# Moving background dequantisation further into the middle layers, and running the last feed-forward by token halves, in a four-layer transformer kernel

## The reference, cut to what matters

```python
x = x + L0_xattn(layernorm(x), ctx)   # 16 heads of 96, 64 context keys + 256 own keys per batch
x = x + L0_ffn(layernorm(x))          # silu(gate/128) * up, 512 -> 1376 -> 512, truncated to int8 twice
x = x + L1_xattn(layernorm(x), ctx)   # one head, softmax(x ctx^T) ctx
x = x + L1_ffn(layernorm(x))          # 64 experts of rank 8, 16 taken per token by a router
x = x + L2_xattn(layernorm(x), ctx)   # as layer 1, with Wq, Wk and biases
x = x + L2_ffn(layernorm(x))          # 3 experts 512 -> 512 -> 512 (tanh, gelu, silu), gated per token
x = x + L3_xattn(layernorm(x), ctx)   # RMS norm with a weight ln_w, 32 heads of 16, grouped keys
x = x + L3_ffn(layernorm(x))          # silu(x dq1^T) * (x dq2^T), then dq3^T; 512 -> 1376 -> 512
...
def nf4_quant_dequant(w):             # dq1..3: blocks of 64 share a maximum; 16 code values
    absmax = jnp.max(jnp.abs(flat), axis=1, keepdims=True)
    idx = jnp.searchsorted(bounds, flat / absmax)
    return (NF4_CODE[idx] * absmax).reshape(shape)
```

## Time and profile before

| | |
|---|---|
| median of 3 runs | 1513.26 us (1510.02 to 1513.64) |
| profiled execution | 1513.1 us, span of its instructions 1511.4 us |
| mean granted TensorE clock | 0.949 |
| TensorE busy | 1366.7 us, 90% of the span |
| VectorE busy | 1002.1 us, 66% |
| GpSimd busy | 328.1 us, 22% |

### The profile page before, as it was taken

The page is one execution under the profiler, slowest core; times in us unless marked ns, Lnnn a source line. Parts: engine busy times, 40 slices in busy tenths (PEclk is TensorE's granted clock), DMA queues, the critical chain, the costliest instruction groups (busy, mean ns, idle before and its releaser), DMA issues.

```text
span 1511.4 us, 18615 instructions
## 1 busy us (share of the span) xinstructions
PE 1366.7 (90%) x6429; PEld 1055.8 (70%) x6429; DVE 1002.1 (66%) x2200; ACT 474.3 (31%) x1004; POOL 328.1 (22%) x187
## 2 busy tenths in 40 slices
PE   6689999999999989997797889778999899999998
PEld 5467676777676766886675676556887677778886
DVE  3577878767878667876988667675446777444242
ACT  3333334333324233341344141322221443321010
POOL 4101211112111111342224140214443230012120
PEclk9889999999999999999899799879999999899999
DMA  4412433323322222332322220100112000011001
GB/s 153 144 39 77 112 116 111 107 77 95 90 80 78 68 77 83 86 113 86 109 81 82 85 84 1 56 29 16 43 54 70 28 29 2 1 49 63 25 20 56
DMA packets 112559, 104.86 MB, mean 69 GB/s; under 512 B 14674, under 2 KB 84194, under 8 KB 112466
## 3 DMA queue, kind: packets, MB, share of 16 engines
q1 hardware_dynamic: 111954, 102.81, 23.2%
q0 software_dynamic: 512, 0.85, 0.2%
HBM read 92.79 MB, written 10.82 MB: 69 GB/s over the span
## 4 chain that ended last, share of the span: by engine, by line
PE 67%; DVE 18%; DMA 4%; issue 3%; ACT 3%; SPq 3%; POOL 2%; ACTq 0%; DVEq 0%
PE bank L1724 49%; PE bank L2093 5%; PE bank L1818 4%; DVE nf_y L1664 4%; PE bank L2028 2%; PE bank L2048 2%; PE bank L1808 2%; POOL slots L858 2%; DVE xn L1238 1%; SPq L807 1%; PE bank L1751 1%; SPq L792 1%; ACT slots L951 1%; PE bank L2037 1%; DVE nf_w L1658 1%
## 5 line engine op out<-in xcount | busy, mean ns | idle before, releaser
L858 POOL TENSOR_TENSOR slots<-staging,slots 128x1024 fp32r<-128x1024 f32 (+5 forms) x114 | 269.0, 2364 | 1025.7 <-ACT slots L951 1025.7
L1724 PE MATMUL bank<-xT,slots 128*128 128x512 f32 (+1 forms) x1920 | 462.0, 398 | 4.5 <-DVE xT L1247 3.2
L1724 PEld LDWEIGHTS bank<-xT,slots 128*128 128x128 f32 (+1 forms) x1920 | 349.0, 183 | 103.5 <-issue 10.8
L1664 DVE TENSOR_SCALAR nf_y<-nf_w 128x512 fp32r<-128x512 f32 (+2 forms) x495 | 254.1, 550 | 21.1 <-PE bank L2093 20.0
L951 ACT ACTIVATE slots<-staging 128x1024 fp32r<-128x1024 f32 (+5 forms) x114 | 115.2, 1018 | 251.1 <-PE bank L1724 217.5
L2093 PE MATMUL bank<-nf_y,nf_d 128*128 128x512 f32 (+2 forms) x495 | 160.9, 418 | 36.2 <-DVE nf_y L1664 20.5
L1724 PE MATMUL bank<-slots,h 128*128 128x512 f32 (+1 forms) x728 | 178.9, 406 | 0.7 <-POOL slots L858 0.7
L1724 PEld LDWEIGHTS bank<-slots,h 128*128 128x128 f32 (+1 forms) x728 | 141.3, 195 | 36.3 <-issue 1.8
L2093 PEld LDWEIGHTS bank<-nf_y,nf_d 128*128 128x128 f32 (+1 forms) x495 | 92.1, 192 | 75.0 <-DVE nf_y L1664 39.1
L985 ACT ACTIVATE e<-bank,mx 128x320 f32<-128x320 f32 x128 | 66.4, 523 | 227.4 <-DVE mx L1275 225.3
L1294 DVE TENSOR_TENSOR x<-bank,x 128x512 f32<-128x512 f32 x56 | 38.7, 692 | 112.7 <-PE bank L1724 112.7
(11 more groups left out here) (250 smaller groups left out, 1673.4 us busy)
## 6 DMA issues: line engine op xcount, KB each, us to landing
staging<-in_L_wqkT SPq DMA_DIRECT2D x16, 480.0 KB, 3.6
nf_out<-nf_w SPq DMA_DIRECT2D x30, 256.0 KB, 2.7
staging<-nf_out SPq DMA_DIRECT2D x30, 256.0 KB, 2.9
staging<-in_L_woT SPq DMA_DIRECT2D x16, 384.0 KB, 3.7
staging<-in_L_w SPq DMA_DIRECT2D x12, 512.0 KB, 3.7
nf_r<-nf_rcp SPq DMA_DIRECT2D x40, 128.0 KB, 3.1
nf_a<-nf_max SPq DMA_DIRECT2D x40, 128.0 KB, 3.5
xn<-in_L_w SPq DMA_DIRECT2D x20, 256.0 KB, 3.7
```

What stands on the lines that cost most here:

```text
L858: g.tensor_tensor(lo, split_source(i), hi.bitcast(FP32), ALU.subtract).then_inc(*sig.mark("weight_low", i))
L1664: v.tensor_scalar(nf_y[0:rows, i % STAIR_RING, 0:size], w_, bound, first, compare, ALU.mult)\
L1724: ins = mm(dst, l_, r_, start=begin and i == 0, stop=end and i == len(passes) - 1)
```

## The change

- `BACKGROUND_END` moves from `down0`(1, 1, 0) to `turn`(4, 1), behind the second attention layer's last `b1`. A `QUIET` stretch from `route1`(0) to `down0`(1, 0, 0) is added, and `down0`(1, ...) gets less room.
- `down0`'s part 0 runs by pairs of blocks over all four tiles, not by tiles over six blocks.
- `hid2`(0, 0 to 2, 0), products of the first expert, move up between the steps of the second attention's softmax. `size2`, the reduction that stood at the end of `turn`(5, half), becomes a step of its own. The buffer `m2` changes its place, so that `hid2`'s results do not fall on it; the biases `b1c` are loaded in layer 0, and `lnw` with the expert's second biases.
- `turn`(6, 0) goes before the last `out2`, `stats`(6, 1) before `k3` and `v3`; the head mask is made at `out2`(0, 0), the cleared `vd3` at `turn`(6, 1).
- `up3`(0, 0) and (1, 0) go into the last rounds of the third attention. The last FFN then takes half 0 through all 11 blocks and after it half 1; every chunk is loaded twice, `h3` is half as large, `down3`(half, part) runs over blocks outside and its four tiles inside. `stats`(7, 1) and `turn`(7, 1) move between the `up3` of half 0.
- The output is stored tile by tile.

```diff
...
-BACKGROUND_END = ("down0", 1, 1, 0)
+BACKGROUND_END = ("turn", 4, 1)
...
-QUIET = {("down0", 1, 1, 1): ("c2",), ("pv1", 1, 2): ("turn", 3, 1), ("route1", 1): ("gate1", 5), ("b1", 7): ("turn", 4, 1),
+QUIET = {("route1", 0): ("down0", 1, 0, 0), ("down0", 1, 1, 1): ("c2",), ("pv1", 1, 2): ("turn", 3, 1), ("route1", 1): ("gate1", 5), ("b1", 7): ("turn", 4, 1),
...
-    steps += [("down0", 0, part, t) for part in range(2) for t in range(TPH)] + [("stats", 2, 0)]
+    steps += [("down0", 0, 0, c) for c in range(3)] + [("down0", 0, 1, t) for t in range(TPH)] + [("stats", 2, 0)]
...
-    steps += [("down0", 1, part, t) for part in range(2) for t in range(TPH)] + [("stats", 2, 1)]
+    steps += [("down0", 1, 0, c) for c in range(3)] + [("down0", 1, 1, t) for t in range(TPH)] + [("stats", 2, 1)]
...
-              ("probs1", 2, 2), ("probs1", 2, 3), ("raw_gate2", 0), ("pv1", 2, 2), ("pv1", 2, 3), ("stats", 5, 1)]
+              ("size2", 0),
+              ("hid2", 0, 0, 0), ("probs1", 2, 2), ("probs1", 2, 3), ("raw_gate2", 0), ("pv1", 2, 2), ("hid2", 0, 1, 0), ("pv1", 2, 3), ("stats", 5, 1),
+              ("hid2", 0, 2, 0)]
...
-    steps += [("gate2", 0), ("hid2", 0, 0, 0), ("hid2", 0, 1, 0), ("turn", 5, 1), ("hid2", 0, 2, 0), ("raw_gate2", 1),
-              ("hid2", 0, 3, 0), ("gate2", 1)]
+    steps += [("gate2", 0), ("hid2", 0, 3, 0), ("turn", 5, 1), ("size2", 1), ("raw_gate2", 1), ("gate2", 1)]
...
-        steps += [("out2", e, t) for t in range(TPH, TILES)]
+        steps += [("out2", e, t) for t in range(TPH, TILES - 1)] + [("turn", 6, 0)] * (e == MOE - 1) + [("out2", e, TILES - 1)]
...
+    steps += [("stats", 6, 1)]
...
-    steps += [("turn", 6, 0), ("stats", 6, 1)]
...
                 steps.append(("turn", 7, 0))
         if n + 2 < len(units):
             steps.append(("keys3", n + 2, *units[n + 2]))
+        if len(units) <= n < len(units) + 2:
+            steps.append(("up3", n - len(units), 0))
     steps += [(step, len(units) - 1, *units[-1]) for step in ("back3", "low3")]
-    steps += [("o3", TILES - 2), ("o3", TILES - 1), ("stats", 7, 1)]
+    steps += [("o3", TILES - 2), ("o3", TILES - 1)]
     if only == 7:
         return steps
     half_f = (FT + 1) // 2
-    steps += [("up3", 0, 0), ("turn", 7, 1), ("up3", 0, 1)]
-    steps += [("up3", f, hf) for f in range(1, half_f) for hf in range(2)]
-    steps += [("down3", 0, t) for t in range(TILES)]
-    steps += [("up3", f, hf) for f in range(half_f, FT) for hf in range(2)]
-    steps += [("down3", 1, t) for t in range(TILES)]
+    steps += [("up3", f, 0) for f in range(2, half_f)] + [("down3", 0, 0), ("up3", half_f, 0), ("stats", 7, 1), ("up3", half_f + 1, 0), ("turn", 7, 1)]
+    steps += [("up3", f, 0) for f in range(half_f + 2, FT)] + [("down3", 0, 1)]
+    steps += [("up3", f, 1) for f in range(half_f)] + [("down3", 1, 0)]
+    steps += [("up3", f, 1) for f in range(half_f, FT)] + [("down3", 1, 1)]
     return steps
...
-          "pv3": 1.3, "o3": 2.6, "up3": 2.6, "down3": 4}
+          "pv3": 1.3, "o3": 2.6, "up3": 5.2, "down3": 15}
...
-        return (6, 1)[step[2]]
+        return ((8, 1), (2, 1))[step[1]][step[2]]
...
-        h3 = sb("h3", [P, 2, (FT + 1) // 2, TOK], F32R, l)
+        h3 = sb("h3", [P, 2, (FT + 1) // 2, HALF], F32R, l)
...
-        for lo, hi in ((0, half_f), (half_f, FT)):
-            ffn_up(("up3",), nf_cols(0), nf_cols(1), lo, hi)
-            ffn_down(("down3",), lambda f, w: nf_out[2][f][0:w], lo, hi)
+        for hf in range(2):
+            for lo, hi in ((0, half_f), (half_f, FT)):
+                ffn_up(("up3", hf), nf_cols(0), nf_cols(1), lo, hi)
+                ffn_down(("down3", hf), lambda f, w: nf_out[2][f][0:w], lo, hi)
...
-                                     ("gbr", gbr[:, 0:MOE], a["L2_gb"].partition_broadcast(P))])
+                                     ("gbr", gbr[:, 0:MOE], a["L2_gb"].partition_broadcast(P)),
+                                     ("b1c", b1c[:], a["L2_b1"])])
...
+                elif kind == "out2" and args == (0, 0):
...
+                elif kind == "turn" and args == (6, 1):
+                    pool.wait_ge(*sig.when("normalised", (6, TILES - 1)))
...
-                w, n = fwidth(f), 2 * f + hf
+                w, n = fwidth(f), hf * FT + f
...
-                    act.wait_ge(*sig.when("back3_low", 15))
+                    act.wait_ge(*sig.when("out2_product", (MOE - 1, TILES - 1)))
+                    act.wait_ge(*sig.when("x_done", (6, 1)))
...
-                if layer == 5:
-                    dve.wait_ge(*sig.when("normalised", (layer, hf * TPH + TPH - 1)))
-                    v.tensor_reduce(ab[:, hf * TPH:(hf + 1) * TPH], xn[:], AX.X, ALU.add, apply_absolute_value=True)\
-                        .then_inc(*sig.mark("strength", hf))
...
+            def size2(hf):
+                dve.wait_ge(*sig.when("normalised", (5, hf * TPH + TPH - 1)))
+                v.tensor_reduce(ab[:, hf * TPH:(hf + 1) * TPH], xn[:], AX.X, ALU.add, apply_absolute_value=True)\
+                    .then_inc(*sig.mark("strength", hf))
...
             def up3(f, hf):
-                w, n = fwidth(f), 2 * f + hf
-                cs = slice(hf * HALF, (hf + 1) * HALF)
+                w, n = fwidth(f), hf * FT + f
                 fi = f % half_f
                 dve.wait_ge(*sig.when("silu3", n))
                 dve.wait_ge(*sig.when("up3_product", (f, hf, 1)))
-                if f >= half_f:
-                    dve.wait_ge(*sig.when("down3_product", (0, TILES - 1)))
-                if n == 0:
-                    dve.wait_ge(*sig.when("o3_product", TILES - 1))
+                if f == half_f:
+                    dve.wait_ge(*sig.when("down3_product", (hf, 0, TPH - 1)))
+                if f == 0 and hf:
+                    dve.wait_ge(*sig.when("down3_product", (0, 1, TPH - 1)))
                 link(v.tensor_tensor(g3[0:w, n % 3], psum(("up3", f, hf, 1))[0:w], g3[0:w, n % 3], ALU.mult))
-                link(v.tensor_copy(h3[0:w, 0, fi, cs], g3[0:w, n % 3]))
-                v.tensor_tensor(h3[0:w, 1, fi, cs], g3[0:w, n % 3], h3[0:w, 0, fi, cs].bitcast(FP32), ALU.subtract)\
+                link(v.tensor_copy(h3[0:w, 0, fi], g3[0:w, n % 3]))
+                v.tensor_tensor(h3[0:w, 1, fi], g3[0:w, n % 3], h3[0:w, 0, fi].bitcast(FP32), ALU.subtract)\
                     .then_inc(*sig.mark("h3_low", n))
-            def down3(part, t):
-                if part:
-                    dve.wait_ge(*sig.when("down3_added", (0, t)))
-                add_to_x("down3", (part, t), t, psum(("down3", part, t))[:])
+            def down3(hf, part):
+                for t in range(TPH):
+                    if part:
+                        dve.wait_ge(*sig.when("down3_added", (hf, 0, t)))
+                    add_to_x("down3", (hf, part, t), hf * TPH + t, psum(("down3", hf, part, t))[:])
...
-            def down0(hf, part, t):
-                user = ("down0_product", (hf, part, t))
-                lo, hi = (0, half_f) if part == 0 else (half_f, FT)
-                pe.wait_ge(*sig.when("h0_done", hf * FT + hi - 1))
-                if part == 0:
-                    open_bank[t] = claim(("down0", hf, t), ("dsign0", hf * TPH + t))
-                pairs = [([h0[0:fwidth(f), f, t * P:(t + 1) * P]], down_chunk(("down0", hf), f, 0, user)) for f in range(lo, hi)]
-                product(open_bank[t][:], pairs, begin=part == 0, end=part == 1).then_inc(*sig.mark(*user))
+            def down0(hf, part, i):
+                user = ("down0_product", (hf, part, i))
+                blocks, tiles = ((2 * i, 2 * i + 1), range(TPH)) if part == 0 else (range(half_f, FT), (i,))
+                if (part, i) == (0, 0):
+                    for t in tiles:
+                        open_bank[t] = claim(("down0", hf, t), ("dsign0", hf * TPH + t))
+                pe.wait_ge(*sig.when("h0_done", hf * FT + blocks[-1]))
+                for t in tiles:
+                    pairs = [([h0[0:fwidth(f), f, t * P:(t + 1) * P]], down_chunk(("down0", hf), f, 0, user)) for f in blocks]
+                    ins = product(open_bank[t][:], pairs, begin=(part, i) == (0, 0), end=part == 1)
+                ins.then_inc(*sig.mark(*user))
...
-            def down3(part, t):
-                user = ("down3_product", (part, t))
+            def down3(hf, part):
                 lo, hi = (0, half_f) if part == 0 else (half_f, FT)
-                pe.wait_ge(*sig.when("h3_low", 2 * hi - 2 + t // TPH))
-                bank = claim(("down3", part, t), ("down3_added", (part, t)))
-                pairs = [([h3[0:fwidth(f), q, f % half_f, t * P:(t + 1) * P] for q in range(2)], down_chunk(("down3",), f, lo, user))
-                         for f in range(lo, hi)]
-                product(bank[:], pairs).then_inc(*sig.mark(*user))
+                tiles = [claim(("down3", hf, part, t), ("down3_added", (hf, part, t))) for t in range(TPH)]
+                for f in range(lo, hi):
```

(45 more changed lines are left out.)

7 lines of the change are left out of this document (3 added, 4 removed).

## The result

The changed kernel takes 1490.5 us (median of four runs, 1483.3 to 1500.3) beside 1512.3 (1510.0 to 1513.6). The ratio is 0.9866, 95% interval [0.9829, 0.9903]: faster by 20 us. I had forecast 1480, 33 us less, in a range of 1463 to 1501. The profiled execution is the slowest of the four (1500.3), so its span shows only 12.9 us of the difference; single stretches compare better than the whole.

A forecast was written before the change was run, and what follows sets the result against it. Bound: TensorE's work, its gaps and the slower-clocked matmuls behind them. Sum: 1513.1 - 22.2 + 6 - 2 - 1 - 5 - 5 - 5 + 2 - 0.8 = 1480.1 us; range 1463 to 1501.

The forecast's parts named there:

- 817 to 868: Stretch in us around `down0`(1): with 23 sums moved away and waits mostly gone, 22.2 us saved, bounds 8 and 25.
- Rival B: `down0`(1) not relieved because its weights come late in place of the sums: saving 8, 1494 us; chance 0.15.
- 868 to 975: Stretch in us receiving 48 moved comparisons, VectorE's load 87%: 6 us lost, bounds -3 and +20.
- rival A: Moved background stalls layers 1 and 2 through VectorE's load or SyncE's loads, costing 20 us: 1494 us; chance 0.20.
- 660 to 743: Stretch in us with `down0`(0): density of comparisons stays, earlier release of weights saves 1 us, bounds 0 and 4.
- 100 to 660: Early stretch in us, 28.2 us idle: 21 comparisons fewer of 392 save 2 us.
- First expert: Its `hid2` products fill waits beside the second attention: 5 us saved of 14.8 idle, bounds 0 and 10.
- layer 3's order: Masks, norm weight and order around layer 3: waits for `lnw` and before the turn go, net 5 us saved.
- `turn`(7,1) -2: In the last FFN, `stats`(7,1) stands behind an `up3`'s VectorE operations, so the turn waits: cost 2 us, bounds 0 and 4.
- the prediction's second sum, 1482.4: Total in place of 1480 if an added GpSimd split stops the chain of `stats`(7,1) for its whole 2.4 us.
- The last FFN's supply: Loading and splitting all weights twice, 17 more chunks, lies beside matmuls (5.5 us a chunk, supply 3.2): cost 0.
- rival D: Doubled weights hold the last FFN, `up3` matmuls waiting for splits; at 6.8 us a chunk 1524 us; chance 0.05.

The follow-up runs named there:

- e1: Changed kernel with the background's end mark, its QUIET stretch and `down0`'s room as before; 1493.6 us, ratio 0.9905.
- e2: Kernel before with only the background's new end mark, the new QUIET stretch and less room in `down0`(1); 1502.0 us, ratio 0.9951.
- e12: Changed kernel with one load replacing 8 to 10 for scales and for maxima per third-matrix item, values not the reference's; 1480.0 us, ratio 0.9775.
- e10: Changed kernel with room 4 in place of 8 for the steps of `down0`(0)'s part 0; 1474.2 us, ratio 0.9749.
- e8: Changed kernel without the QUIET stretch from `route1`(0) to `down0`(1,0,0); 1483.9 us, ratio 0.9820.
- e3: Changed kernel with `stats`(7,1) before `down3`(0,0) and `turn`(7,1) right behind it; 1488.4 us, ratio 0.9856.
- e4: Changed kernel with the last FFN, its chunks, hidden buffer, fill and output transfers as before; 1488.9 us, ratio 0.9865.
- e6: Changed kernel with `hid2`(0, 0 to 2, 0) back behind `stats`(5,1), `size2` kept apart; 1497.6 us, ratio 0.9909.

## Why the prediction was right or wrong

By its terms, in us saved; measured are the stretches of the two profiled executions, where the changed one is the slowest of its four.

- **817 to 868: forecast 22.2.** Right. 51 us became 21.7; less 5.3 for the moved sums, 24. No wait of L2093, clock 1.00. Rival B is refuted, `down0`(1) got its weights in time. Only behind it, `z1` waits 8.50 us for its split where it waited 6.40 before.
- **868 to 975: forecast 6 lost, the step that failed.** From the first `k2` to `turn`(5,0) 120.3 us (868.51 to 988.77) became 151.6: 31.4 more, 11.0 of them sums, so 20 lost. This is rival A, at its price, and e1 and e2 show that the moved background makes it. I had argued from a density averaged over 100 us, and of SyncE I had counted 8.8 us of issues an item, from a row of the last block; the item before it has 11.7 us of issues (5.85 and 5.83) and takes the queue 18 us with its waits. e12 shows 5 to 7 us of the 20 as loads. The rest I put down to comparisons ahead of `zg` and `xn` on VectorE, to jobs that the QUIET stretches in these layers push together, and to the slower matmuls behind each gap; this is argued, and their shares stay open.
- **660 to 743: forecast 1 saved.** From `turn`(1,1) to `turn`(2,0) it is 0.7, so the number is right, but by luck: the pairs of blocks set the same jobs in three clumps of 8, and the longest wait for a sum grew from 4.66 us to 10.00, while a wait of 6.37 us for `xn` at `turn`(2,0) went away. e2, with the old `down0`, is only 3.3 us shorter in this part. e10, e8 and e12 show that 7 to 18 us could be had here, which the forecast didn't see.
- **100 to 660: forecast 2.** `turn`(1,0) starts 3.5 us sooner, but e3, e4 and e6, with the changed kernel's steps up to there, lie between 448.2 and 455.2: the term is neither shown nor refuted.
- **First expert 5, layer 3's order 5.** Right: 10.9 together, 4.1 and 6.8 by e6.
- **Attention's end 5, `turn`(7,1) -2, last transfer 0.8.** The sum is -0.5 and not 3.8. At `turn`(7,1) the mechanism was right and the term was mis-sized: its wait is 3.03 us, inside the bound, but with it and the lower clock behind it e3 took away some 6 us, for the 2 that I had set. This is nearer to the prediction's second sum, 1482.4, in which the term is 4.4. VectorE's and GpSimd's timelines of the changed kernel:

```profile
1363.84 2.33 DVE L1206 TENSOR_TENSOR rt<-rs 128x4 f32<-128x4 f32 x1
...
1367.19 1.92 DVE L1241 TENSOR_SCALAR xn<-x,mv,rs 128x512 f32<-128x512 f32 x4
```
```profile
1363.79 2.36 POOL L858 TENSOR_TENSOR slots<-staging,slots 128x1024 fp32r<-128x1024 f32 x1 [3.82 <-ACT slots L953]
```

  A VectorE operation with two inputs, 0.16 us otherwise, takes 2.33 us: it starts 0.05 us behind a split and ends with it, at 1366.2. By the Trainium skill ("SBUF — State Buffer", "Who interferes with whom") a VectorE instruction with two inputs in SBUF and a GpSimd instruction that reads SBUF exclude each other, the first to issue for its whole length, and the trace agrees. Without it the wait of 3.03 us would have been some 0.9, an estimate (3.03 less 2.33 - 0.16).
- **The last FFN's supply: forecast 0.** Right; rival D is refuted. In the groups of 1315 to 1495 us 27 splits stand beside the matmuls, TensorE waits for none of them, and VectorE's two-input operation has gone from 1.174 us to 1.767 at no cost:

```profile
L858 POOL TENSOR_TENSOR slots<-staging,slots 128x1024 fp32r<-128x1024 f32 x27 | 65.6, 2435 | 133.1 <-ACT slots L953 133.0
...
L1622 DVE TENSOR_TENSOR h<-g,h 128x512 fp32r<-128x512 f32 x18 | 31.8, 1767 | 0.6
```

The forecast, 33 us, was 13 too high by the ratio. By the two traces, whose spans differ by 12.9 us, it was 20 too high: 14 are the failed step, 4 come from `turn`(7,0) to the end, and 4 from the stretches ahead of `down0`(1) (4.6 us sooner, less 5.7 for the 25 sums moved out of them, for a forecast of 3); some 3 were won back in `down0`(1) and the fourth stretch. The three other executions of the changed kernel were 10 to 17 us shorter than the traced one; no trace shows where.
